# Macaron block on one core: query weights made in halves, the last batch's sums on two engines, fewer filler matmuls

## The chip, the cores and the metric

The kernel runs on one core of one Trainium2 chip. The metric is the device time of one execution in microseconds, lower is better; of a kernel the median of its runs is given. The names of the engines are those of the profile: PE is TensorE, DVE VectorE, ACT ScalarE, POOL GpSimd, SP the engine that only starts transfers. Each engine works through its own list of instructions in order and waits on semaphores for the others.

## What is computed

The input x is 16 batches of 512 rows of 128 numbers in float32. Three sublayers follow each other, each with a residual:

```
x = x + 0.5 * ffn(layernorm(x))      # one 128x128 weight, rounded to int4, plus a rank-16 term and a bias
x = x + attention(layernorm(x))
x = x + 0.5 * ffn(layernorm(x))      # the same weights again

attention: q = x Wq (16 heads of 64);  c = x Wkv_down (32 wide);  k = c Wk_up;  v = c Wv_up
           softmax(q k' / 8, causal) v, then Wout
```

Since k is c times a matrix of 64 columns per head, q k' is x (Wq Wk_up') c'. The kernel makes the product Wq Wk_up' once per head (128 x 32), the "query weights", and likewise Wv_up Wout. Scores are then products with only 32 contracted latents.

## The kernel before

**Rounds.** Every engine runs `one_round(t)` for t = -2 to 16. A round has up to four parts: `prep` makes the first sublayer, queries and keys of batch t+2; `top` finds row maxima of batch t+1; `attend` does scores and exponentials of batch t; `end` does the rest of batch t-1 (normalising, output projection, last sublayer, store). A round is cut into 44 slots u (`SCORES`), one score tile each. The order inside a round is written out by hand: the tables at the top of the file (`WEIGH_AT`, `ADD_AT`, `PROJECT_AT` and so on) give the slot at which an engine comes to each piece; a number over 43 lies in the next round. Rounds -2 and -1 have no scores, so only semaphores pace them; they use the `OPENING_` tables. In round 14 and later no new batch is prepared, round 15 attends the last batch, and round 16 only ends it.

**The opening.** PE rounds and centres the int4 weight (L780, then `w_ffn` by DVE, L1068). `front_unit(0)` transposes x of batch 0 (L929), ACT copies it (L718), `front_unit(1)` multiplies by `w_ffn` (L932), DVE adds the residual (L1202). Then `transpose_weights` transposes Wq and Wk_up in 8 pairs (L786, L787), ACT's `keep_transposed` copies them to SBUF (L663, L664), `query_products` multiplies (L796), and DVE's `keep_queries` scales them into `w_query` (L1074), makes a rounded copy `query_high` (L1078) and the remainder `query_low` (L1079). ACT fills rows of the query stack with the causal mask (`mask_queries`, L656): two groups at the start, one ahead of `keep_transposed`, one behind it; then it normalises x (`normalise`, L710). `front_unit(2)` transposes the normalised x (L929), ACT and DVE split it in `x_high` and `x_low` (L1221); `front_unit(3)` makes the keys and `front_unit(4)` to `(7)` the queries of the four groups of heads, three matmuls each (L941 to L943). POOL meanwhile fills `keys` with masks (L508, L522). In round -1 follow the next batch's first units, the value weights (L804, L812) and the first maxima (L903, with DVE's L1127).

**A batch's attention.** The 16 heads are four groups g of 4; a group has four key tiles j. PE makes scores (L839, L843), ACT takes exponentials (L697) into `first_probs` (j = 0) or `later_probs`. `weigh_latents(g, j)` multiplies them with the latents (L868); with j = 0 it first adds the row sums of the first 128 queries (L852). The other row sums come from `totals`, the sum of the probabilities over j: three adds per group, of 1536, 1024 and 512 columns, and `weigh_ones(g)` sums them over the partitions (L852). The adds of a batch run on POOL (`add_probs`, L593), those of the last batch all on DVE (`last_add`, L1144). An exponential that overwrites a buffer waits for the add that read it two groups before; `weigh_ones` waits for its group's three adds. ACT copies a group's result out of PSUM (`read_y`, L703).

**A batch's end.** When all four `weigh_ones` are done DVE inverts the sums (L1156), spreads them (L1163, in round 16 L1173) and POOL multiplies (`scale_y`, L600, four times; in round 16 `close_y`, L582, and DVE L1178). `project_out` (L985) waits for all of it, then come x2 (L1209, in round 16 L1183 and L1189), its transposes (`tail_unit(1)`, L998), the copy (L751), the last product (`tail_unit(2)`, L1001), POOL's bias and deviation (L637, L550, L552), and DVE's last sum (L1216) ahead of the store.

**Filler.** In round 16 PE also runs matmuls whose result nobody reads: `stay_busy_by_columns(BUSY[0])` ahead of each `weigh_ones` there (L969), `stay_busy(BUSY[1])` ahead of the first projection, `BUSY[2]` ahead of `tail_unit(1)`, `BUSY[3]` ahead of `tail_unit(2)` (L962); each of them is two matmul instructions of 256 columns.

Of the kernel before, what the change touches and what calls it, by code (L numbers as in the profile page):

```python
# [11 lines left out]
P = 128  # L12
# [123 lines left out]
LAST_WEIGH_AT = [[12, 17, 17, 17], [31, 31, 31, 31], [37, 37, 37, 37], [44, 49, 52, 65]]  # L136
LAST_ONES_AT = [31, 40, 44, 46]
# [56 lines left out]
def ones_at(b, g):  # L194

    return (LAST_ONES_AT if b == B - 1 else ONES_AT)[g]


def macaron_block(nc, x, wq, wkv_down, wk_up, wv_up, wout, ffn_w, ffn_bias, ffn_a, ffn_b, out):
    ctx = ExitStack()  # L200
    with ctx:
# [73 lines left out]
        w_query = early[:, 0:H * LD].rearrange("p (j o c) -> p j o c", o=2, c=LD)  # L275
# [6 lines left out]
        ring, (aux, score0, score1, y_bank, den_bank) = banks[:RING], banks[RING:]  # L282
        wide_scores = [*ring, score1, score0]
# [198 lines left out]
        def _(pool):  # L482
# [59 lines left out]
            def one_round(t, par):  # L542
# [59 lines left out]
                for u in range(SCORES):  # L602
# [10 lines left out]
                    for off, there in ((-1, end), (0, attend)):  # L613
                        for g in range(G):
                            for turn, at in enumerate(ADD_AT[g]):
                                if there and t + off < B - 1 and at == u - SCORES * off:
                                    add_probs(off, g, turn + 1)
# [25 lines left out]
        def _(act):  # L643
# [15 lines left out]
            def keep_transposed():  # L659

                act.wait_ge(w_pe, 4)
                for i in range(2):
                    nc.scalar.activation(wq_t[:, i * 4:(i + 1) * 4, :].rearrange("p j d -> p (j d)"), ring[i][:], ACT.Copy)  # L663
                nc.scalar.activation(wk_t[:].rearrange("p j c -> p (j c)"), ring[2][:, 0:H // 2 * LD],  # L664
                                     ACT.Copy).then_inc(w_act, 1)

            def keep_values():

                act.wait_ge(w_pe, 6)
                nc.scalar.activation(wv_t[:].rearrange("p j c -> p (j c)"), score1[:, 0:H // 2 * LD],  # L670
                                     ACT.Copy).then_inc(w_act, 1)
                act.wait_ge(w_pe, 7)
# [8 lines left out]
            def one_round(t, par):  # L681
# [62 lines left out]
                for u in range(SCORES):  # L744
# [23 lines left out]
        def _(pe):  # L768
# [9 lines left out]
            pe.wait_ge(w_dve, 3)  # L778
            pe.wait_ge(const_made, 6)
            nc.tensor.matmul(score1[:, 0:D], centering[:], quant[:, 1], start=True, stop=True).then_inc(w_pe, 1)  # L780

            def transpose_weights():
# [508 lines left out]
```

## Time and profile before

| | |
|---|---|
| median of 3 runs | 799.28 us (798.09 to 802.14) |
| profiled execution | 799.71 us |
| its span, first to last instruction | 797.5 us |
| PE busy | 764.4 us, 96% |
| DVE busy | 637.3 us, 80% |
| POOL busy | 628.1 us, 79% |
| ACT busy | 509.3 us, 64% |
| mean granted PE clock | 0.988 |

The engines' rows give the time in which each had an instruction running. Idle time of an engine costs only where the chain of waits that ends last goes through it. In the page's 40 slices of 20 us PE shows 9 in nearly all, and less in the first four and in the last two.

### The profile page before, as it was taken

The page shows a single profiled execution, that of the slowest core. Times are in us where ns is not written, and L with a number is a line of the kernel's source. Part 1 is how long each engine was busy: PE and PEld are TensorE (multiplying, and loading weights), DVE is VectorE, ACT ScalarE, POOL GpSimd, SP SyncE. Part 2 cuts the span into 40 slices and gives each one's busy share as a digit, 9 for nine tenths or more (in the row PEclk, how much of TensorE's full clock was granted, in tenths as well). Part 3 has the DMA queues.
Part 4 walks back from the last instruction along what each step waited for, and adds up shares of the span by engine and source line. Part 5 has one row for each costly group of instructions (what it writes and reads, how often), then busy time and mean ns, then how long its engine had stood idle before and what let it go on. Part 6 is the DMA issues. An engine that isn't in the chain of part 4 may idle for free.

```text
span 797.5 us, 20469 instructions
## 1 busy us (share of the span) xinstructions
PE 764.4 (96%) x7520; PEld 587.4 (74%) x7520; DVE 637.3 (80%) x1988; ACT 509.3 (64%) x993; POOL 628.1 (79%) x436
## 2 busy tenths in 40 slices
PE   5689999999999999999999999999999999999897
PEld 3556778778787777778787877878777877857576
DVE  3488878797878878897888879887888888876765
ACT  4365766667657666766757666776767666755660
POOL 4503879888998989888998989889898988878712
PEclk9988999999999999999999999999999999999999
DMA  4457272553627164453616264363626254360101
GB/s 115 95 124 174 53 158 72 120 128 81 162 49 161 46 147 101 107 143 81 154 41 157 65 140 108 89 160 74 148 50 154 72 125 112 81 141 2 29 2 41
DMA packets 81123, 80.97 MB, mean 102 GB/s; under 512 B 16048, under 2 KB 68544, under 8 KB 81024
## 3 DMA queue, kind: packets, MB, share of 16 engines
q1 hardware_dynamic: 80464, 78.47, 42.3%
q10 hardware_dynamic: 560, 1.20, 0.6%
q8 instruction: 60, 0.98, 0.5%
q14 instruction: 39, 0.32, 0.1%
HBM read 9.90 MB, written 8.39 MB: 23 GB/s over the span
## 4 chain that ended last, share of the span: by engine, by line
PE 85%; DVE 6%; SPq 2%; POOL 2%; ACT 2%; issue 2%; DMA 1%; ACTq 0%; DVEq 0%; POOLq 0%
PE bank L868 17%; PE bank L903 15%; PE bank L843 14%; PE bank L839 8%; PE bank L852 8%; PE bank L985 8%; PE bank L941 2%; PE bank L929 2%; SPq L398 2%; PE bank L943 2%; PE bank L942 2%; PE bank L932 2%; PE bank L1001 2%; DVE strip_max L1127 1%; PE bank L946 1%
## 5 line engine op out<-in xcount | busy, mean ns | idle before, releaser
L1127 DVE TENSOR_REDUCE strip_max<-bank 128x8 f32<-128x512 f32 (+1 forms) x384 | 254.2, 683 | 49.2 <-PE bank L903 48.5
L697 ACT ACTIVATE later_probs<-bank 128x512 f32<-128x512 f32 x384 | 216.3, 600 | 67.6 <-PE bank L843 41.9
L697 ACT ACTIVATE first_probs<-bank 128x384 f32<-128x384 f32 (+1 forms) x320 | 157.4, 512 | 139.7 <-PE bank L843 73.8
L593 POOL TENSOR_TENSOR totals<-totals,later_probs 128x1024 f32<-128x1024 f32 x120 | 220.2, 1835 | 11.5
L593 POOL TENSOR_TENSOR totals<-first_probs,later_probs 128x1536 f32<-128x1536 f32 x60 | 208.7, 3478 | 23.0 <-ACT later_probs L697 23.0
L903 PE MATMUL bank<-keys,q_stack 118*128 118x512 f32 (+7 forms) x1024 | 214.9, 304 | 3.0 <-DVE maxima L1127 1.2
L903 PEld LDWEIGHTS bank<-keys,q_stack 118*128 118x128 f32 x1024 | 177.7, 192 | 18.3 <-DVE strip_max L1127 3.7
L843 PE MATMUL bank<-q_stack,keys 119*128 119x384 f32 (+1 forms) x448 | 186.1, 424 | 2.8 <-ACT later_probs L697 1.7
L1127 DVE TENSOR_REDUCE maxima<-bank 128x1 f32<-128x512 f32 (+1 forms) x192 | 128.1, 681 | 3.9 <-PE bank L903 3.9
L843 PEld LDWEIGHTS bank<-q_stack,keys 119*128 119x128 f32 x448 | 83.6, 190 | 45.6 <-ACT first_probs L697 16.2
L839 PE MATMUL bank<-q_stack,keys 119*128 119x256 f32 x512 | 113.8, 304 | 0.9 <-DMA q_stack<-max_t 0.7
L839 PEld LDWEIGHTS bank<-q_stack,keys 119*128 119x128 f32 x512 | 82.7, 190 | 28.8 <-ACT later_probs L697 16.1
L868 PE MATMUL bank<-later_probs,lat 128*32 128x384 f32 (+2 forms) x1536 | 98.8, 383 | 0.0
L600 POOL TENSOR_TENSOR y_norm<-y_sb,y_norm 128x512 f32<-128x512 f32 x60 | 79.1, 1328 | 20.5 <-DVE y_norm L1163 20.5
L868 PEld LDWEIGHTS bank<-later_probs,lat 128*32 128x32 f32 x1536 | 43.6, 109 | 54.3 <-issue 35.5
L985 PE MATMUL bank<-w_out,y_norm 128*128 128x128 f32 x512 | 70.0, 281 | 2.9 <-POOL y_norm L600 2.4
L985 PEld LDWEIGHTS bank<-w_out,y_norm 128*128 128x128 f32 x512 | 64.5, 194 | 6.1 <-issue 5.3
L868 PE MATMUL bank<-first_probs,lat 128*32 128x512 f32 x512 | 66.7, 592 | 0.2 <-ACT y_sb L703 0.2
L1163 DVE STREAM_SHUFFLE y_norm<-den_inv 128x128 f32<-128x128 f32 x240 | 54.3, 308 | 0.5
L1231 DVE TENSOR_TENSOR q_low<-bank,q_high 128x512 fp32r<-128x512 f32 x64 | 43.8, 684 | 9.3 <-ACT q_high L729 9.2
L703 ACT ACTIVATE y_sb<-bank 128x512 f32<-128x512 f32 x64 | 38.4, 600 | 19.6 <-PE bank L868 19.6
L852 PE MATMUL bank<-totals,row_ones 128*32 128x128 f32 x1536 | 50.9, 273 | 0.0
(144 smaller groups left out, 889.9 us busy)
## 6 DMA issues: line engine op xcount, KB each, us to landing
q_stack<-q_high SPq DMA_DIRECT2D x252, 128.0 KB, 2.4
q_stack<-q_low SPq DMA_DIRECT2D x128, 128.0 KB, 2.4
x_in<-in_L_attn_x_bld_dram SPq DMA_DIRECT2D x16, 256.0 KB, 3.5
out_dram<-x SPq DMA_DIRECT2D x16, 256.0 KB, 3.5
x_back<-out_dram SPq DMA_DIRECT2D x16, 256.0 KB, 3.1
out_dram<-x2b SPq DMA_DIRECT2D x16, 256.0 KB, 2.3
keys<-keys_staged SPq DMA_DIRECT2D x16, 192.0 KB, 2.9
keys<-keys_staged SPq DMA_DIRECT2D x32, 96.0 KB, 2.8
```

The costliest lines, as they stand in the source:

```text
L593: nc.gpsimd.tensor_tensor(total, first_probs[g % 2][:, :, P:] if j == 1 else total, probs_of(g, j)[:], ALU.add).then_inc(added, 1)
L600: nc.gpsimd.tensor_tensor(y_norm[:, g, :], y_sb[:, g, :], y_norm[:, g, :], ALU.mult).then_inc(y_normed, 1)
L697: nc.scalar.activation(out, score_bank(t, u)[:, 0:heads * cols].rearrange("p (e q) -> p e q", e=heads), ACT.Exp).then_inc(exp_done, 1)
L839: last = nc.tensor.matmul(out, strips(par, KM, OWN[w]), q_stack[par][:, pair:pair + HG, w, of, :], start=True, stop=True)
L843: last = nc.tensor.matmul(bank[:, 0:heads * (n - P)], strips(par, KM, LATER[j]), q_stack[par][:, pair + e:pair + e + heads, 2 * (j + 1):SU ...
L852: last = nc.tensor.matmul(den_bank[e * LD:(e + 1) * LD, 0:P], row_ones[:, row:row + LD], of[:, e, :], start=start, stop=stop)
L868: last = nc.tensor.matmul(y_bank[e * LD:(e + 1) * LD, j * P:L], lat[(par + off) % 2][:, j, :], probs_of(g, j)[:, e, 0:L - P * j], start=(j ...
L903: last = nc.tensor.matmul(bank[:, col:col + n], queries, strips((par + off) % 2, KC, SEEN[w]), start=True, stop=True)
L985: last = nc.tensor.matmul(out_tile(t, i), y_norm[:, g, i * P:(i + 1) * P], w_out[:, g, :], start=(g == 0), stop=(g == G - 1))
L1127: nc.vector.tensor_reduce(out, bank[:].rearrange("q (b k) -> q b k", k=strip), AX.X, ALU.max).then_inc(a_free, 1)
L1163: last = nc.vector.stream_shuffle(y_norm[:, g, i * P:(i + 1) * P], den_inv[:], [g * TT + i] * LD)
L1231: nc.vector.tensor_tensor(q_low[:, g // 2, :, g % 2, :], front_bank(t, QUERY_UNIT + g)[:].rearrange("p (w q) -> p w q", q=HALF_TILE), q_hi ...
```

## The change

Three edits, none of which touches rounds 0 to 14.

In the opening the weights are transposed, copied, multiplied and kept in two halves of four pairs, the products in other banks; `w_query` is gone, `query_high` and `query_low` are both computed from PSUM; the centring matmul is issued behind `front_unit(0)`; and ACT fills both remaining mask groups ahead of the first copy. In the last batch the adds of groups 0 and 1 go to POOL, those of groups 2 and 3 stay on DVE, and the slots of adds, `weigh_latents` and `weigh_ones` are other ones. In round 16 `BUSY[2]` is 0 instead of 9.

```diff
-LAST_WEIGH_AT = [[12, 17, 17, 17], [31, 31, 31, 31], [37, 37, 37, 37], [44, 49, 52, 65]]
-LAST_ONES_AT = [31, 40, 44, 46]
+LAST_WEIGH_AT = [[10, 13, 13, 14], [21, 21, 25, 31], [33, 40, 40, 40], [42, 51, 52, 52]]
+LAST_ONES_AT = [33, 40, 52, 54]
...
-LAST_ADD_AT = [[19, 19, 22], [24, 24, 24], [30, 30, 32], [32, 41, 41]]
-BUSY = [1, 6, 9, 1]
+LAST_ADD_AT = [[10, 22, 22], [22, 24, 25], [28, 29, 34], [40, 40, 42]]
+BUSY = [1, 6, 0, 1]
+POOL_GROUPS = 2
...
+        product_banks = [(y_bank, den_bank), ring[0:2]]
...
-                                if there and t + off < B - 1 and at == u - SCORES * off:
-                                    add_probs(off, g, turn + 1)
+                                if there and (t + off < B - 1 or g < POOL_GROUPS) and u - SCORES * off == add_at(t + off, g, j):
+                                    add_probs(off, g, j)
...
-                            mask_queries(0, EARLY_MASKS)
-                            keep_transposed()
-                            mask_queries(0, EARLY_MASKS + 1)
+                            for g in range(EARLY_MASKS, G):
+                                mask_queries(0, g)
+                            keep_transposed(0)
...
+                    if is_first(t) and u == norm_at[TT - 1]:
+                        keep_transposed(1)
...
                     if is_first(t) and u == 1:
+                        centre_weights()
                         pe.wait_ge(w_dve, 4)
...
-                        pe.wait_ge(w_dve, 6)
+                        pe.wait_ge(w_dve, 6 + (u - QUERY_UNIT) // 2)
...
                     if is_first(t) and u == front_at[1]:
-                        transpose_weights()
-                        query_products()
+                        for half in range(2):
+                            transpose_weights(half)
+                        query_products(0)
+                    if is_first(t) and u == front_at[2]:
+                        query_products(1)
...
+            def keep_queries(half):
+
+                dve.wait_ge(w_pe, 6 + half)
+                js = slice(half * HG, (half + 1) * HG)
+                of = [bank[:, 0:HG * LD].rearrange("p (j c) -> p j c", c=LD) for bank in product_banks[half]]
                 for odd in range(2):
-                    ins = nc.vector.tensor_scalar(w_query[:, :, odd, :], ...
+                    last = nc.vector.tensor_scalar(query_high[:, js, odd, :], of[odd], HD ** -0.5, None, ALU.mult)
+                link(last)
+                for odd in range(2):
+                    last = nc.vector.scalar_tensor_tensor(query_low[:, js, odd, :], of[odd], HD ** -0.5,
+                                                          query_high[:, js, odd, :].bitcast(F32), ALU.mult, ALU.subtract)
...
                     if j == 1:
-                        wait_batch(dve, den_done, t, off, G, max(g - 1, 0))
-                    else:
-                        wait_batch(dve, added, t, off, G * GROUP_ADDS, g * GROUP_ADDS + j - 1)
+                        wait_batch(dve, den_done, t, off, G, g - 1)
+                    wait_batch(dve, added, t, off, G * GROUP_ADDS, g * GROUP_ADDS + j - 1)
```

On DVE `keep_queries(0)` stands where `keep_queries` stood, behind `split_keys`; `keep_queries(1)` stands behind the subtraction that finishes the keys (L1226) and ahead of the first `q_low`.

## Rows read from the trace of the kernel before

**Rows 1.** The page, busy time of each engine over the whole span.

```profile
PE 764.4 (96%) x7520; PEld 587.4 (74%) x7520; DVE 637.3 (80%) x1988; ACT 509.3 (64%) x993; POOL 628.1 (79%) x436
```

**Rows 2.** Timeline of the opening: start us, us, engine, line, operation; idle before in brackets.

```profile
8.92 0.29 DVE L1068 TENSOR_SCALAR w_ffn<-bank 128x128 f32<-128x128 f32 x1 [0.89 <-PE bank L780]
...
10.51 2.05 PE L932 MATMUL bank<-w_ffn,x_t 128*128 128x128 f32 x8 [0.78 <-ACT x_t L718]
...
12.60 1.13 DVE L1202 SCALAR_TENSOR_TENSOR x<-bank,f_rstd,x_in 128x128 f32<-128x128 f32 x4 [3.39 <-PE bank L932]
...
17.23 0.31 PE L787 MATMUL bank<-identity,y_sb 32*128 32x32 f32 x1
...
18.96 1.91 ACT L656 ACTIVATE q_stack<-first_probs 22x2048 fp32r<-22x2048 f32 x1
...
18.99 3.62 PE L796 MATMUL bank<-later_probs 64*128 64x32 f32 x32 [1.45 <-ACT later_probs L664]
20.89 1.65 ACT L710 ACTIVATE xn<-x,f_shift,f_rstd 128x128 f32<-128x128 f32 x4
...
21.78 3.75 POOL L522 MEMSET keys<- 22x2176 f32 x2
...
23.45 2.37 DVE L1078 CAST query_high<-later_probs 128x512 fp32r<-128x512 f32 x1
...
27.30 0.71 PE L941 MATMUL bank<-x_high,wkv_low 128*96 128x512 f32 x1 [3.63 <-DVE x_low L1221]
...
29.51 0.63 PE L943 MATMUL bank<-x_low,query_high 128*128 128x512 f32 x1
...
32.05 0.40 PE L943 MATMUL bank<-x_low,query_high 128*128 128x512 f32 x1
```

**Rows 3.** The same timeline further on, the first maxima on PE.

```profile
42.50 3.87 PE L903 MATMUL bank<-keys,q_stack 118*128 118x512 f32 x12
```

**Rows 4.** Timeline of the last batch, rounds 15 and 16.

```profile
746.84 2.28 ACT L697 ACTIVATE later_probs<-bank 128x512 f32<-128x512 f32 x4 [1.11 <-PE bank L843]
...
748.59 7.50 POOL L600 TENSOR_TENSOR y_norm<-y_sb,y_norm 128x512 f32<-128x512 f32 x4 [4.02 <-DVE y_norm L1163]
...
752.85 3.79 DVE L1144 TENSOR_TENSOR totals<-totals,later_probs 128x1024 f32<-128x1024 f32 x2
...
756.24 1.13 PE L985 MATMUL bank<-w_out,y_norm 128*128 128x128 f32 x8 [2.37 <-POOL y_norm L600]
...
758.41 2.02 DVE L1144 TENSOR_TENSOR totals<-totals,later_probs 128x1024 f32<-128x1024 f32 x2
...
763.95 1.04 PE L868 MATMUL bank<-first_probs,lat 128*32 128x512 f32 x8
...
778.79 1.48 PE L868 MATMUL bank<-later_probs,lat 128*32 128x384 f32 x24
779.04 0.96 DVE L1156 RECIPROCAL den_inv<-bank 128x128 f32<-128x128 f32 x1 [0.70 <-PE bank L852]
```

**Rows 5.** Windows: us, busy (instructions) PE, PEld, DVE, ACT, POOL, granted clock, DMA share, GB/s.

```profile
758.00:760.00 2.00, 2.00 (x10) 2.00 (x9) 1.79 (x3) 0.58 (x2) 0.00 (x0) 0.50 0.00 0
```

**Rows 6.** Groups of POOL by shape: busy us, mean ns, then idle before and its releaser.

```profile
L593 POOL TENSOR_TENSOR totals<-first_probs,later_probs 128x1536 f32<-128x1536 f32 x60 | 208.7, 3478 | 23.0 <-ACT later_probs L697 23.0
L593 POOL TENSOR_TENSOR totals<-totals,later_probs 128x1024 f32<-128x1024 f32 x60 | 143.0, 2383 | 4.9
L600 POOL TENSOR_TENSOR y_norm<-y_sb,y_norm 128x512 f32<-128x512 f32 x60 | 79.1, 1328 | 20.5 <-DVE y_norm L1163 20.5
L593 POOL TENSOR_TENSOR totals<-totals,later_probs 128x512 f32<-128x512 f32 x60 | 77.2, 1287 | 6.6
```

**Rows 7.** The chain of waits at the end: start us, us, what.

```profile
787.42 3.89 PE bank L962 x18
791.30 0.45 PE bank L998 x4
```

**Rows 8.** Timeline of the end, POOL and DVE.

```profile
789.37 1.04 POOL L552 TENSOR_TENSOR t_rstd<-t_var,neg_half 128x4 f32<-128x4 f32 x1
...
793.62 1.12 DVE L1216 SCALAR_TENSOR_TENSOR x2b<-bank,t_rstd,x2b 128x128 f32<-128x128 f32 x4 [5.03 <-PE bank L1001]
```

More of the change, by code:

```diff
@@ L614, in one_round @@
                         for g in range(G):
-                            for turn, at in enumerate(ADD_AT[g]):
-                                if there and t + off < B - 1 and at == u - SCORES * off:
-                                    add_probs(off, g, turn + 1)
+                            for j in range(1, TT):
+                                if there and (t + off < B - 1 or g < POOL_GROUPS) and u - SCORES * off == add_at(t + off, g, j):
+                                    add_probs(off, g, j)
                     if prep and u == rstd_at:
@@ L777, in _, with centre_weights, transpose_weights, query_products @@
             nc.tensor.matmul(score1[:, 0:1], ones[0:1, :], absmax[0:1, 2:3], start=True, stop=True).then_inc(w_pe, 1)
[L778 to L782, printed above, removed]
-                pe.wait_ge(w_loaded, 2 * DMA)
-                for j in range(H // 2):
-                    nc.tensor.transpose(ring[j // 4][:, (j % 4) * P:(j % 4 + 1) * P], wq_in[:, j * P:(j + 1) * P], identity[:])
-                    last = nc.tensor.transpose(ring[2][:, j * LD:(j + 1) * LD], wk_in[:, j * P:(j + 1) * P], identity[0:LD, 0:LD])
+            def centre_weights():
+                pe.wait_ge(w_dve, 3)
+                pe.wait_ge(const_made, 6)
+                nc.tensor.matmul(score1[:, 0:D], centering[:], quant[:, 1], start=True, stop=True).then_inc(w_pe, 1)
+            def transpose_weights(half):
+                pe.wait_ge(w_loaded, 2 * DMA)
+                q_bank, k_bank = (ring[0], ring[2]) if half == 0 else (ring[1], score0)
+                for n in range(HG):
+                    j = half * HG + n
+                    nc.tensor.transpose(q_bank[:, n * P:(n + 1) * P], wq_in[:, j * P:(j + 1) * P], identity[:])
+                    last = nc.tensor.transpose(k_bank[:, n * LD:(n + 1) * LD], wk_in[:, j * P:(j + 1) * P], identity[0:LD, 0:LD])
                 last.then_inc(w_pe, 1)
-            def query_products():
-                pe.wait_ge(w_act, 1)
-                for j in range(H // 2):
+            def query_products(half):
+                pe.wait_ge(w_act, half + 1)
+                for n in range(HG):
                     for odd in range(2):
                         rows = slice(odd * HD, (odd + 1) * HD)
-                        last = nc.tensor.matmul(ring[odd][:, j * LD:(j + 1) * LD], wq_t[rows, j, :], wk_t[rows, j, :],
-                                                start=True, stop=True)
+                        last = nc.tensor.matmul(product_banks[half][odd][:, n * LD:(n + 1) * LD], wq_t[rows, half * HG + n, :],
+                                                wk_t[rows, half * HG + n, :], start=True, stop=True)
                 last.then_inc(w_pe, 1)
@@ L1259, in one_round @@
                         for g in range(G):
-                            for turn, at in enumerate(LAST_ADD_AT[g]):
-                                if there and t + off == B - 1 and u - SCORES * off == at:
-                                    last_add(off, g, turn + 1)
+                            for j in range(1, TT):
+                                if there and t + off == B - 1 and g >= POOL_GROUPS and u - SCORES * off == add_at(t + off, g, j):
+                                    last_add(off, g, j)
             rounds(dve, one_round)
```

34 lines of the change are left out of this document (15 added, 19 removed).

## The prediction

> **What bounds the kernel now.** I read the page's busy shares first, then the chain of waits at both ends, then the timeline there with all engines side by side, and the windows for the clock. PE is busy 96% of the span [rows 1], and the middle, rounds 0 to 14, is left alone by the change. So the question is only the first 42 us, up to the first maxima [rows 3], and the last 50. In the opening the chain changes engines at each step, so a step saved there moves all that follows. The reader is to see in [rows 2] that PE waits 1.45 us for ACT's copies ahead of the products, that ACT then fills a mask (18.96 to 20.87) while the normalisation stands behind it, and that DVE has `query_high` in hand for 2.37 us beside POOL's memset; only then come x_low and, after 3.63 us of PE's waiting, the keys. In the last batch PE waits 2.37 us for POOL's scalings [rows 4] and then works at half clock, 0.50 (1.2 instead of 2.4 GHz) in the window of [rows 5]; behind that it has no gap until the inversion at 779.04. At the very end 18 filler matmuls stand on the chain for 3.89 us [rows 7].
>
> **Part 1, the opening.** I count from start to start.
> (a) Today x is transposed behind the centring matmul, and L932 starts at 10.51, released by the copy of x. In the new order the transposes stand in front of it, in a gap where PE waits for DVE; the copy is over by about 8.4, since ACT's first two masks end at 7.7. The next one late is `w_ffn`, ready at 9.21 [rows 2]. So L932 starts at 9.3: 1.2 us saved, and ends at 11.35.
> (b) The eight transposed pairs end at 17.54, which is 4.98 behind the end of L932 (12.56). They are not fewer: 11.35 + 5.0 = 16.35. ACT has done both masks by 8.4 + 2 x 1.91 = 12.2, ahead of the end of the first half at 13.6, so moving the second mask forward is free, and the first half's copies (about 0.9) lie beside PE's second half. PE goes straight on: first products 1.8 (half of 3.62), to 18.2; transposes of x about 1.0, to 19.2. The normalised x is there, because the mask no longer stands in front of it: its inputs come 1.2 earlier than today's 17.3, so 16.1 + 1.65 = 17.8. The second half's copies come behind it, 0.9, to 18.7; second products 1.8, to 21.0.
> (c) DVE keeps the first half at 18.2 with four instructions of 128 columns. The trace has no such instruction from PSUM into these buffers; L1202 has the same operation and width at 0.28 a step, L1068 is 0.29, the upper bound is the whole of today's 0.77 + 2.37 + 0.69 = 3.8 for both halves. I take 0.29 each, 1.2 with the link: done at 19.4, ahead of x_high (19.9). x_low ends at 20.6. So the keys start at 21.0 instead of 27.30: 6.3 us. With the upper bound (1.9 per half) x_low is over at 20.8, and nothing changes here.
> (d) The keys take 1.3 (PE) + 0.2 + 0.6 (ACT) + 0.7 (DVE), and only then DVE keeps the second half: 23.8 + 1.2 = 25.0. The third and fourth group's queries wait for it. Six matmuls of 512 columns follow at 0.43 to 0.24 each, depending on the clock: today they are 0.43 apart (0.63 long) until 30.4 and 0.24 apart (0.40 long) behind it [rows 2]. That is the end at 27.6 or at 26.5, against 32.45 today: 4.8 to 5.9 saved. I take 5.4. Bounds: 3.5, if the second half costs 1.9 and PE is still cold; 6.3, the gain at the keys.
> The Trainium skill says in "TensorE: Matmul & The Clock Gate", Part 1, that the slow clock is the default and steady activity releases it; by that rule the unbroken run of PE from 19.2 on would bring the fast clock by the queries (the 5.9 end), while from the rows alone I keep the middle.
> (e) Who is late next: from there ACT's last q_high, its four DMA issues, the latents' copy, the next batch's two units, the value weights and the first maxima [rows 3] follow each other as today. POOL's masks begin with the deviation, 1.2 earlier, and end at 27.7 instead of 28.9; they are needed ahead of the first maxima at 37. The loaded weights have landed (Wk_up, the later, near 9.7) ahead of the first transpose near 10.9. The transfers of queries and keys move with their sources. I let the 5.4 pass in full: rounds -1 and later have the same work in the same order.
>
> **Part 2, the last batch.** Before: DVE adds groups 0 and 1 beside POOL's scalings of batch 14. Four scalings take 7.50, 1.88 each against 1.33 on average [rows 4, 6], and DVE's adds of 1024 and 512 columns take 3.79 beside them, 2.02 without [rows 4]. So the two engines hold each other up.
> After, on POOL: the first add needs the exponential that ends at 747.45 (first of the four at 746.84 [rows 4]); 747.5 + 3.48, then four scalings of 1.28 to 1.33, is 756.1 to 756.3. That is where they end today (756.09): the add costs what the contention gives back. Then 2.38 + 1.29 for group 0 (760.0) and 3.48 + 2.38 + 1.29 for group 1 [rows 6]: 767.2. Behind the adds are queued the bias and the deviation of batch 14 (2.6, needed only at the round's last slots).
> On PE: `weigh_latents(1, 0)` and `(1, 1)` now stand in front of the projection. Their inputs come by 753.5 and 754.7 (ACT's order kept, 0.5 to 0.6 each), and they fill 0.35 + 0.86 + 0.64 = 1.85 of the wait. Against that `weigh_latents(3, 1..3)` now stand in front of the last sums instead of behind them (the 1.48 at 778.79 in [rows 4]): plus 1.43. The half clock: before, PE stood still 2.37 in one piece and was then at 0.50 for 3.41 us; half of this, 1.7, is lost time. After, what is left of the wait is about 1.3 in pieces. I take it that the clock stays up: minus 1.7. Sum: 779.04 - 1.85 + 1.43 - 1.7 + 0.1 (later projection) = 777.0, so 2.0 saved. Ends: 0.3 if the half clock stays, and 3.8 if the whole of the wait and of the clock were given back and the moved weighings cost nothing.
> Do the adds keep up? Group 1's sums are asked for on PE at about 769.2 and ready at 767.2: slack 2.0. Group 2's adds on DVE wait for POOL's last (767.2, since they now wait for the count) and run to 771.1; group 3's (1.76 + 2.02) wait for the exponentials of the round's end and run to 775.3, asked for at 776.3: slack 1.0. The end of batch 14 on DVE (L1216) comes behind them, off the chain.
> The Trainium skill has the rule for this in "SBUF — State Buffer", Who interferes with whom: a DVE instruction with two SBUF inputs and a GpSimd instruction that reads SBUF exclude each other for whole instructions. It agrees with the 3.79 against 2.02 above; it speaks against sharing one batch's sums between these two engines, and would matter here only for POOL's 1.29 bias add beside DVE's group 2, which has slack.
>
> **Part 3, the filler.** Behind x2 (DVE, 787.74) PE's transposes would start at 787.8 and not at 791.3 [rows 7]; copy, one filler, the last product: 787.8 + 0.6 + 0.7 + 1.2 = 790.3. Next late is POOL's deviation, which ends at 790.41 [rows 8]. DVE's last sum starts at 790.46 instead of 793.62: 3.15 saved. If the clock fell without the filler, the last product would take one more microsecond: 2.2. That is the lower end; there is no upper one beyond 3.15, as POOL sets it.
>
> **Sum.** 5.4 + 2.0 + 3.15 = 10.5 against the profiled execution, whose 799.71 is the span 797.5 and 2.2 around it: 789.2. That execution lies 0.43 over the median, so for a median 788.7. I say 789.0.
>
> **Rivals.**
> R1, the half clock stays in the last batch, or comes at another place of the rounds whose clock the shift disturbs: 1.7 less, 790.7. For it: PE still has gaps from 753 to 756; against it: they are shorter than the 2.37 today.
> R2, the opening's gain goes into a new wait, say the copies or the second half's chain (keys, ACT, DVE, then the kept half): only (a) and what the mask costs today, some 1.2 + 1.4, are left. 789.0 + 2.8 = 791.8. For it: the second half's queries hang on a chain of four engines; against it: PE's own work up to the keys, 21.0, is counted whole.
> R3, the last batch gives nothing, because its sums now end behind the weighings and their adds: 791.0.
> R4, the other side: POOL sets the pace of the last batch. Its adds of two groups are 14.3 us. If DVE's reads held POOL up as the scalings held up DVE (3.79 against 2.02, 1.88 times), they would take 26.9, 12.6 more; past the slack of 2.0 all of it is on the chain through the exponentials of group 3 and the sums: 10.6 more, and a PE that waits that long comes back at half clock, 1.7 more. 789.0 + 12.3 + the 2.0 not gained = 803.3; it begins to cost at 2.0 us of lateness and makes the kernel slower than before from about 12. Against it: between 756 and 767 DVE has little with two inputs in SBUF now.
> R5, both clocks fall out well and the queries take the 5.9: 786.5 to 788.
>
> **How the numbers follow.** Forecast 0.48, R1 0.16, R2 0.12, R3 0.08, R4 0.04, R5 0.08, and 0.04 for no gain that can be told. About 0.5%, 4 us, is what a measurement can tell from no change, so faster means below 795.3. The range takes in R1, R2, R3, R5 and combinations of two of the low ends (opening 3.5 and half clock: 792.7): 785.5 to 794.0. Faster 0.90, same 0.06, slower 0.04.
>
> **What would show it.** Keys' L941 near 21 and the last query matmul by 26.5 to 27.6; normalisation at about 16.2; no long CAST on DVE; the first L903 near 37. In the last batch: four L600 of about 1.3 each, L985 at the same distance from the round's start as now, no 0.50 in the windows behind it, L1156 about 2.0 nearer to it. At the end no L962 ahead of L998, and L1216 started by POOL's L552. The prediction is wrong if the first maxima come less than 3.5 us earlier, or if PE is seen waiting for adds (L593 or L1144) in round 15.

## The result and the profile after

The changed kernel took 789.95 us in the median of its runs (788.35 to 792.54) against 799.3 us, a ratio of 0.9881 with a 95% interval of 0.9843 to 0.9920. Run again later beside more runs of the kernel before, it gave 0.9910 (0.9888 to 0.9932). The forecast was 789.0 us in a range of 785.5 to 794.0. The profiled execution took 789.15 us, its span is 787.4 us; they are 10.6 and 10.1 below those of the kernel before. One of the ten runs of opening_only below took 4030.57 us and is left out of its ratio.

The line numbers moved: L932 is now L946, L796 is L809, L941 to L943 are L955 to L957, L903 is L916, L843 and L839 are L856 and L852, L868 is L881, L852 (sums) is L865, L593 is L599, L600 is L606, L1144 is L1161, L1156 is L1173, L985 is L999, L998 is L1012, L1216 is L1233.

The opening in the timeline of the changed kernel (start us, us, engine, line, operation; idle before in brackets), to be held against [rows 2]:

```profile
9.22 2.08 PE L946 MATMUL bank<-w_ffn,x_t 128*128 128x128 f32 x8 [0.38 <-DVE w_ffn L1085]
...
13.73 0.60 ACT L670 ACTIVATE later_probs<-bank 128x512 f32<-128x512 f32 x1 [1.64 <-PE bank L800]
...
16.06 1.65 ACT L717 ACTIVATE xn<-x,f_shift,f_rstd 128x128 f32<-128x128 f32 x4 [1.56 <-POOL f_shift L575]
...
16.21 1.92 PE L809 MATMUL bank<-later_probs 64*128 64x32 f32 x16
...
18.17 0.49 DVE L1093 TENSOR_SCALAR query_high<-bank 128x128 fp32r<-128x128 f32 x2 [3.49 <-PE bank L809]
18.70 0.49 DVE L1096 SCALAR_TENSOR_TENSOR query_low<-bank,query_high 128x128 fp32r<-128x128 f32 x2
19.11 1.92 PE L809 MATMUL bank<-later_probs 64*128 64x32 f32 x16
...
20.96 0.74 PE L955 MATMUL bank<-x_high,wkv_low 128*96 128x512 f32 x1
...
26.26 0.40 PE L957 MATMUL bank<-x_low,query_high 128*128 128x512 f32 x1
```

L946 now waits for `w_ffn` and no longer for the copy of x. The first half's copy (13.73) lies beside the second half's transposes, PE goes from them to the first products without waiting, and neither the second products nor the keys (20.96) have a wait in brackets: from 16.2 to the keys PE is its own limit. DVE has kept the second half at 24.94, and the third group's queries start behind it at 24.99, after a wait of 0.22. The last query matmul ends at 26.66 instead of 32.45. Further on, the first maxima, to be held against [rows 3]:

```profile
36.64 4.17 PE L916 MATMUL bank<-keys,q_stack 118*128 118x512 f32 x12
```

The last batch, to be held against [rows 4]:

```profile
740.97 2.28 ACT L704 ACTIVATE later_probs<-bank 128x512 f32<-128x512 f32 x4 [1.11 <-PE bank L856]
...
741.65 3.50 POOL L599 TENSOR_TENSOR totals<-first_probs,later_probs 128x1536 f32<-128x1536 f32 x1 [2.94 <-ACT later_probs L704]
...
745.11 5.00 POOL L606 TENSOR_TENSOR y_norm<-y_sb,y_norm 128x512 f32<-128x512 f32 x4
...
748.67 1.04 PE L881 MATMUL bank<-first_probs,lat 128*32 128x512 f32 x8
749.53 0.83 PE L881 MATMUL bank<-later_probs,lat 128*32 128x384 f32 x8
...
750.29 1.16 PE L999 MATMUL bank<-w_out,y_norm 128*128 128x128 f32 x8
...
761.38 2.73 DVE L1161 TENSOR_TENSOR totals<-first_probs,later_probs 128x1536 f32<-128x1536 f32 x1 [3.15 <-POOL totals L599]
...
768.23 2.02 DVE L1161 TENSOR_TENSOR totals<-totals,later_probs 128x1024 f32<-128x1024 f32 x2
...
772.03 0.96 DVE L1173 RECIPROCAL den_inv<-bank 128x128 f32<-128x128 f32 x1 [0.74 <-PE bank L865]
```

The four scalings take 5.00, not 7.50, and end at 750.1 with the first add of 3.50 in front of them. Counted from batch 14's inversion (746.45 before, 740.58 after) the projection starts at +9.79 before and at +9.71 after: the same place. The last inversion is at +32.59 before and +31.45 after. The windows after the projection (us, then busy us of PE, PEld, DVE, ACT, POOL, granted clock, DMA share, GB/s), against [rows 5]:

```profile
752.00:754.00 2.00, 2.00 (x20) 1.34 (x19) 0.00 (x0) 1.53 (x4) 1.86 (x3) 1.00 0.00 0
754.00:756.00 2.00, 2.00 (x19) 2.00 (x19) 0.00 (x0) 1.02 (x3) 2.00 (x1) 1.00 0.00 0
```

And the end, against [rows 8]:

```profile
782.34 1.04 POOL L558 TENSOR_TENSOR t_rstd<-t_var,neg_half 128x4 f32<-128x4 f32 x1
783.51 1.12 DVE L1233 SCALAR_TENSOR_TENSOR x2b<-bank,t_rstd,x2b 128x128 f32<-128x128 f32 x4 [1.94 <-POOL t_rstd L558]
```

PE is no longer the one that DVE's last sum waits for; POOL's deviation is. From inversion to that sum it is 11.48 now, 14.58 before.

By milestones of the two profiles the 10.1 us of span are: 5.9 up to the first maxima (5.5 at the first score of batch 0, 65.20 against 59.66, and 5.9 at batch 14's inversion), 1.1 in the last batch, 3.1 at the filler.

### The profile page after: what moved, and what is told of

Its sections match the earlier page's. It is cut to its first block, busy times and chain, and to the rows that moved or that the text cites. A ratio compares the mean times of both kernels' runs of the same rounds, so it can differ in the third digit from the quotient of the medians.

```text
span 787.4 us, 20439 instructions
## 1 busy us (share of the span) xinstructions
PE 762.5 (97%) x7502; PEld 583.2 (74%) x7502; DVE 626.7 (80%) x1986; ACT 509.3 (65%) x994; POOL 642.0 (82%) x442
## 4 chain that ended last, share of the span: by engine, by line
PE 88%; DVE 5%; ACT 2%; POOL 1%; issue 1%; SPq 1%; DMA 1%; ACTq 0%; POOLq 0%; DVEq 0%
PE bank L881 18%; PE bank L916 16%; PE bank L856 14%; PE bank L852 8%; PE bank L865 8%; PE bank L999 7%; PE bank L955 2%; PE bank L943 2%; PE bank L956 2%; PE bank L957 2%; PE bank L946 2%; PE bank L1015 2%; DVE strip_max L1145 1%; SPq L404 1%; PE bank L960 1%
## 5 line engine op out<-in xcount | busy, mean ns | idle before, releaser
L599 POOL TENSOR_TENSOR totals<-totals,later_probs 128x1024 f32<-128x1024 f32 x124 | 227.3, 1833 | 11.9
L599 POOL TENSOR_TENSOR totals<-first_probs,later_probs 128x1536 f32<-128x1536 f32 x62 | 215.7, 3479 | 25.9 <-ACT later_probs L704 25.9
L916 PE MATMUL bank<-keys,q_stack 118*128 118x512 f32 (+7 forms) x1024 | 215.2, 305 | 2.5 <-DVE maxima L1145 1.2
L916 PEld LDWEIGHTS bank<-keys,q_stack 118*128 118x128 f32 x1024 | 178.5, 193 | 17.4 <-DVE strip_max L1145 2.8
L856 PE MATMUL bank<-q_stack,keys 119*128 119x384 f32 (+1 forms) x448 | 185.8, 423 | 2.7 <-ACT later_probs L704 1.7
L856 PEld LDWEIGHTS bank<-q_stack,keys 119*128 119x128 f32 x448 | 83.0, 189 | 45.7 <-ACT first_probs L704 16.0
L852 PE MATMUL bank<-q_stack,keys 119*128 119x256 f32 x512 | 114.1, 305 | 0.3 <-ACT later_probs L704 0.2
L852 PEld LDWEIGHTS bank<-q_stack,keys 119*128 119x128 f32 x512 | 82.6, 190 | 29.9 <-ACT later_probs L704 17.2
L881 PE MATMUL bank<-later_probs,lat 128*32 128x384 f32 (+2 forms) x1536 | 99.5, 383 | 0.0
L606 POOL TENSOR_TENSOR y_norm<-y_sb,y_norm 128x512 f32<-128x512 f32 x60 | 76.5, 1287 | 16.6 <-DVE y_norm L1180 16.6
L881 PEld LDWEIGHTS bank<-later_probs,lat 128*32 128x32 f32 x1536 | 43.1, 109 | 54.2 <-issue 35.3
L999 PE MATMUL bank<-w_out,y_norm 128*128 128x128 f32 x512 | 69.1, 278 | 1.5 <-POOL y_norm L588 1.5
L999 PEld LDWEIGHTS bank<-w_out,y_norm 128*128 128x128 f32 x512 | 63.1, 191 | 5.9 <-issue 3.8
L881 PE MATMUL bank<-first_probs,lat 128*32 128x512 f32 x512 | 66.7, 592 | 0.3 <-ACT y_sb L710 0.2
L865 PE MATMUL bank<-totals,row_ones 128*32 128x128 f32 x1536 | 50.9, 273 | 0.0
L736 ACT ACTIVATE q_high<-bank 128x512 fp32r<-128x512 f32 x64 | 38.4, 599 | 16.5 <-PE bank L957 16.2
```

Of the source, the lines that this page charges most:

```text
L599: nc.gpsimd.tensor_tensor(total, first_probs[g % 2][:, :, P:] if j == 1 else total, probs_of(g, j)[:], ALU.add).then_inc(added, 1)
L606: nc.gpsimd.tensor_tensor(y_norm[:, g, :], y_sb[:, g, :], y_norm[:, g, :], ALU.mult).then_inc(y_normed, 1)
L852: last = nc.tensor.matmul(out, strips(par, KM, OWN[w]), q_stack[par][:, pair:pair + HG, w, of, :], start=True, stop=True)
L856: last = nc.tensor.matmul(bank[:, 0:heads * (n - P)], strips(par, KM, LATER[j]), q_stack[par][:, pair + e:pair + e + heads, 2 * (j + 1):SU ...
L865: last = nc.tensor.matmul(den_bank[e * LD:(e + 1) * LD, 0:P], row_ones[:, row:row + LD], of[:, e, :], start=start, stop=stop)
L881: last = nc.tensor.matmul(y_bank[e * LD:(e + 1) * LD, j * P:L], lat[(par + off) % 2][:, j, :], probs_of(g, j)[:, e, 0:L - P * j], start=(j ...
```

## The experiments

Each edit is against the kernel before or the changed one, as it says. A ratio is that of its runs to runs of the kernel before on the same chip.

**opening_only**: the changed kernel with the last batch's tables, its adds' engine and the fillers put back.

```diff
-BUSY = [1, 6, 0, 1]
+BUSY = [1, 6, 9, 1]
-POOL_GROUPS = 2
+POOL_GROUPS = 0
...                # and LAST_WEIGH_AT, LAST_ONES_AT, LAST_ADD_AT as before
```

> The kernel with the opening's edits alone; last batch and filler as before. Theory (each engine step moved what follows): the first maxima start at 36.6, 5.9 earlier than 42.5, the first score of batch 0 5.5 earlier, and the span is 797.5 - 5.5 = 792.0. Rival (the rounds behind give part of it back, through transfers or another clock pattern in rounds -1 and 0): first maxima as above, but a span above 794.5. Third possibility, that part of the gain seen at the end of the changed kernel is not the opening's: span under 791.

Measured: 795.02 us, ratio 0.9943 (0.9919 to 0.9967), which is 4.5 us (2.6 to 6.5). In its profile the first maxima start at 38.01 and the first score at 62.76, the span is 794.4: 1.4, 3.1 and 2.4 us later than expected. Up to the keys it was all as in the changed kernel (below). What differs is the clock: the table further down shows 22.4 us at half clock up to that score in this profile against 11.5 in the changed kernel's. So I had taken the accident of one pair of profiles for the size of the term. The profiled run is also the longest of the nine that count, and the record, which has a mean granted clock for every run, shows the same link in all of them: they go from 796.65 us at 0.981 to 791.80 us at 0.991.

**last_batch_only**: the kernel before with the last batch's three tables, POOL's adds of groups 0 and 1, and DVE's additional wait.

> The kernel with the last batch's edits alone (adds of groups 0 and 1 on POOL, the new slots of weighings and sums), opening and 9 fillers as before. Theory: POOL's scalings take 5.0 instead of 7.5 and end where they ended; the half clock behind the projection is gone; the inversion starts 1.1 to 1.4 earlier (between batch 14's and the last inversion 31.2 to 31.5 instead of 32.6). Rival, that the gain of 1.1 in the changed kernel is the shifted clock windows and not the new order: then here the half clock stays, and the distance is over 32.3.

Measured: 798.04 us, ratio 0.9977 (0.9957 to 0.9996), 1.8 us (0.3 to 3.4). The inversions are 31.47 apart (744.65, 776.12), no half clock behind the projection, scalings 5.00. As the theory had it.

**filler_only**: the kernel before with `BUSY = [1, 6, 0, 1]`.

> The kernel with BUSY[2] = 0 alone: 9 filler matmuls less ahead of the last transposes. Theory: DVE's last sum is released by POOL's deviation and starts 3.1 earlier (from inversion to last sum 11.5 instead of 14.6), PE's clock stays at 1.00 to the last product; span 794.4. Rival, that PE drops to half clock without the fillers and the last product ends behind POOL: 12.4, span 795.3.

Measured: 796.26 us, ratio 0.9949 (0.9929 to 0.9969), 4.1 us (2.5 to 5.7). From inversion to last sum 11.50, the clock at 1.00 from round 1 until 792.7. The chain of waits of this run (start us, us, what) shows who took over; in [rows 7] it was 3.89 of PE's fillers:

```profile
786.78 0.83 POOL x2b L637
787.61 0.41 issue
788.02 0.23 POOL t_var L550
788.25 0.04 issue
788.29 1.09 POOLq L201
```

This run held a surprise elsewhere. Its last batch is that of the kernel before, to the instruction, with the same wait of 2.37 ahead of the projection, and yet the clock did not fall behind it:

```profile
756.81 1.13 PE L985 MATMUL bank<-w_out,y_norm 128*128 128x128 f32 x8 [2.37 <-POOL y_norm L600]
757.70 0.48 PE L839 MATMUL bank<-q_stack,keys 119*128 119x256 f32 x2
758.01 1.05 PE L985 MATMUL bank<-w_out,y_norm 128*128 128x128 f32 x8
```

The second projection takes 1.05 here and 1.85 in the profile of before:

```profile
757.45 1.85 PE L985 MATMUL bank<-w_out,y_norm 128*128 128x128 f32 x8
```

Here the clock stays at 1.00, and the inversions are 30.98 apart (747.02, 778.00) instead of 32.59. So the half clock costs 1.6 us there, and it is not in every run.

**slots_only**: the kernel before with the new slots of weighings and sums, all adds left on DVE.

```diff
-LAST_WEIGH_AT = [[12, 17, 17, 17], [31, 31, 31, 31], [37, 37, 37, 37], [44, 49, 52, 65]]
-LAST_ONES_AT = [31, 40, 44, 46]
+LAST_WEIGH_AT = [[10, 13, 13, 14], [21, 21, 25, 31], [33, 40, 40, 40], [42, 51, 52, 52]]
+LAST_ONES_AT = [33, 40, 52, 54]
```

> The kernel with the new slots of weighings and sums in the last batch, but all adds on DVE at their old slots. It tells the two edits of the last batch apart. Theory (contention): POOL's scalings still take about 7.5 beside DVE's adds, the projection starts at the same place, and since the wait is filled with the two weighings here too, the half clock goes and the inversion comes 1 to 1.4 earlier: the adds' new engine is worth nothing by itself. Rival, that moving the adds to POOL is what counts: the distance between the two last inversions stays at 32.3 to 32.6 here.

Measured: the scalings take 7.53, the projection is 9.81 behind the inversion, the next inversion 31.52 (749.26, 780.78), against 31.45 and 31.47 with the adds on POOL. Between the inversions the engine of the adds is worth nothing by itself. The whole took 800.1 us, ratio 0.9999 (0.9978 to 1.0019), so in the median the slots alone show no gain. That is 2.1 us more than last_batch_only, more than the last batch of the two profiles can explain. A part is the clock: seven of these ten runs have a mean of 0.981 to 0.985, only three of the ten of last_batch_only 0.982 to 0.984, and in both kernels the runs with the lower clock are mostly the longer ones. Whether the rest is chance or the adds' engine, no run here shows.

**psum_read_only**: the kernel before, `query_high` and `query_low` made from PSUM in one piece.

```diff
-                    ins = nc.vector.tensor_scalar(w_query[:, :, odd, :],
...
-                link(nc.vector.tensor_copy(query_high[:], w_query[:]))
-                nc.vector.tensor_tensor(query_low[:], w_query[:], query_high[:].bitcast(F32),
...
+                    last = nc.vector.tensor_scalar(query_high[:, :, odd, :], of[odd], HD ** -0.5, None, ALU.mult)
...
+                    last = nc.vector.scalar_tensor_tensor(query_low[:, :, odd, :], of[odd], HD ** -0.5,
+                                                          query_high[:, :, odd, :].bitcast(F32), ALU.mult, ALU.subtract)
```

> Of the opening only this: DVE makes query_high and query_low from PSUM, in one piece, so no copy or cast between SBUF buffers is left. In the profile of before the cast took 2.37 us beside POOL's memset, in three later profiles of the same code 0.51. Theory (the cast and the memset exclude each other, and who comes first at the memset's end decides): the four instructions take 1.5 to 1.7 in all, the keys' first matmul starts 2.9 to 3.1 behind the end of the products, as in the runs in which the cast won (3.0) and not as before (4.7); in the median a gain of 0 to 1 us, within the noise. Rival, that reading from PSUM is itself slow or also held: the four instructions take over 2.5, keys start over 4 behind the products.

The long cast of [rows 2] had turned out to be an accident too. In last_batch_only, slots_only and filler_only, whose opening is that of the kernel before, it is short. The last of them, in its timeline:

```profile
21.98 4.04 POOL L522 MEMSET keys<- 22x2176 f32 x2
22.88 0.75 DVE L1074 TENSOR_SCALAR later_probs<-bank 128x256 f32<-128x256 f32 x2 [6.72 <-PE bank L796]
23.66 0.51 DVE L1078 CAST query_high<-later_probs 128x512 fp32r<-128x512 f32 x1
24.21 0.69 DVE L1079 TENSOR_TENSOR query_low<-later_probs,query_high 128x512 fp32r<-128x512 f32 x1
```

POOL's two memsets start at 21.98 and about 23.85. The cast starts at 23.66, inside the first. Here it gets its turn between the two: it takes 0.51, and POOL's pair takes 4.04. In the kernel before the second memset came first: cast 2.37, pair 3.75. In both the cast starts 0.23 to 0.24 before the end of the first memset (1.91 each), so the times do not show what decides. Measured with psum_read_only: 0.76 + 0.76 for the four instructions, the keys 2.55 behind the end of the products (23.39 to 25.94; I had expected 2.9), ratio 0.9986 (0.9964 to 1.0008), not to be told from no change.

**order_only**: the kernel before, with the centring behind the transposes of x and both mask groups ahead of the copies.

> Of the opening only the orders: centring matmul behind the transposes of x, both mask groups ahead of the copies; weights in one piece, kept through w_query as before. Theory: L932 starts at 9.3 (1.2 earlier) and the normalisation about 16.1 to 16.5 or right behind the copies at 18.5, but the products still end at 21.4 and the keys start 24.2 to 24.5 (against 25.65 in runs without the long cast): 1.2 to 1.4 us. Rival, that the mask's place was the chief cost: 2 us or more.

Measured: the start of the whole moves by up to 1.2 us between runs (the first data land differently), so the opening is read from DVE's first instruction, which waits for them (3.82 to 4.99 in the runs here). From it to the keys it is 20.29, against 21.50 with the cast short: 1.21, that is the centring's place. The mask's place adds nothing here, where the products of the weights in one piece end at 22.26 and the keys wait for what DVE does behind them; whether the mask behind the copies would hold up the halves was not tried. Ratio 0.9978 (0.9954 to 1.0001).

**fill_the_wait**: the kernel before, with unread matmuls in round 15's wait.

```diff
+                        if t == B - 1:
+                            for _ in range(5):
+                                nc.tensor.matmul(aux[:, 0:L // 2], identity[:], w_out[:, 0:2, :], start=True, stop=True)
```

> The kernel before plus ten filler matmul instructions of 256 columns (unread, into the output's bank) on PE in round 15 while it waits for the first projection. Theory (the 1.6 us between the last two inversions, 32.6 with and 31.0 without a half clock, are the clock alone): no 0.50 behind the projection, distance 31.0, end 1.6 earlier than in a run that has the half clock; the projection itself starts where it did. Rival, that fillers delay the projection or the clock falls all the same: 32.6 or more.

Measured: 2.32 of fillers, the projection at +9.72, no half clock, the inversions 30.93 apart (747.37, 778.30). Ratio 0.9981 (0.9962 to 1.0000), 1.5 us (0 to 3.0). With filler_only, which has neither the fillers nor the half clock and 30.98, it shows that the clock alone makes the 1.6, and that without it the old order is 0.5 us faster than the new one.

**all_on_pool**: the changed kernel with `POOL_GROUPS = 4`.

> The changed kernel with all twelve adds of the last batch on POOL. It prices the slack. Theory: POOL has group 1's adds by 761.2 and needs 7.15 per group more instead of 3.8: group 2's and the bias work end about 771, group 3's about 778.5 instead of 770.3, so the last sums wait and the inversion comes at about 779, 7 later than in the changed kernel: span 794 to 795. Rival, that the adds have more slack than I think: under 3 us later.

Measured: 799.11 us, ratio 0.9999 (0.9980 to 1.0018), span 796.3; the inversions are 39.33 apart, 7.9 more than in the changed kernel (7 expected). PE waits for the adds (who waited for whom, us in total, times, longest), and its clock falls behind it, from 776.1 for 6.8 us:

```profile
PE bank L865 <- POOL totals L599: 6.9, 1, 6.9
```

Two groups fit on POOL, four use up the whole gain of the change.

**after_again**: the changed kernel.

> The changed kernel once more, with more runs beside those of before. Theory (opening 4.5 in the median, since the long cast and the clock windows fall differently from run to run, last batch 1 to 2, filler 3.1): median 8.5 to 10 below before. The halves' milestones as in its first profile: keys at most 12.0 behind the start of L946, last two inversions 31.4 to 31.5 apart, inversion to last sum 11.5.

Measured: 792.12 us against 798.46, ratio 0.9910 (0.9888 to 0.9932), 7.2 us (5.4 to 8.9): below the 8.5 to 10 that I had expected, though the interval reaches into it. The three parts, each measured alone, add up to 10.4 (4.5, 1.8 and 4.1), and the first measurement of the whole gave 9.4; the intervals are too wide to say that the parts get in each other's way. Keys 11.73 behind L946, inversions 31.44 apart, 11.51 to the last sum. First score at 62.66, 3.0 later than in the first profile of the same program.

**no_sum_filler**: the changed kernel with `BUSY = [0, 6, 0, 1]`.

> The changed kernel with BUSY[0] = 0: the 16 filler matmul instructions of 0.86 us per group ahead of the last two weigh_ones are gone. Theory (the adds of group 3 on DVE have about 1.0 of slack to the last sums): of 1.7 only 1.0 comes back, then PE waits for L1161; inversions 30.4 to 30.5 apart, and 0.8 to 1.0 in the median. Rival, that without them the clock falls: 32 or more.

(A unit of `BUSY[0]` is eight matmul instructions of 512 columns, L983, once for each of the two groups; only the units of the other three are two of 256 columns.) Measured: 790.86 us, ratio 0.9891 (0.9869 to 0.9913), which can't be told from after_again by its interval; inversions 30.72 apart, 0.7 less, and PE waits 0.8 for L1161. The adds do limit, a little earlier than I had said.

**warm_opening**: the changed kernel, with unread matmuls in PE's waits of the opening.

```diff
+                    fill = {(-2, front_at[LATENT_UNIT]): 6, (-1, front_at[0]): 5, (-1, front_at[1]): 2}.get((t, u), 0)
+                    for _ in range(fill):
+                        nc.tensor.matmul(ring[2][:, 0:P], identity[:], identity[:], start=True, stop=True)
```

> The changed kernel with 13 unread matmuls of 128 columns on PE, into a free bank, in the three waits between the last query and the second unit of batch 1 (1.4, 1.2 and 0.7 us). Theory (the half clock of 31 to 41 us comes from PE standing still there, and costs what PE then does on the chain, some 2 us up to the first maxima): no 0.50 from 31 on, L946 of round -1 1.1 instead of 2.1, first maxima 1.5 to 2.5 nearer to the end of the queries (8.0 to 8.9 instead of 10.4), 1 to 2.5 in the median. Rival, that the clock falls all the same, or that DVE (which sets the pace of round -1) eats the gain: under 0.5 in the first score of batch 0.

Measured: 789.00 us, ratio 0.9884 (0.9862 to 0.9906). The median is 3.1 below after_again; the two intervals overlap, so the gain rests on the milestones. Windows of after_again (columns as above):

```profile
24.00:31.00 7.00, 4.16 (x14) 2.64 (x12) 5.05 (x17) 2.55 (x5) 4.13 (x13) 0.93 0.68 150
31.00:41.00 10.00, 8.67 (x60) 6.71 (x60) 4.18 (x16) 3.55 (x8) 3.72 (x6) 0.54 0.95 216
```

and of warm_opening:

```profile
24.00:31.00 7.00, 6.92 (x44) 5.72 (x42) 5.00 (x17) 2.85 (x6) 4.68 (x13) 1.00 0.68 150
31.00:41.00 10.00, 8.67 (x72) 5.99 (x70) 7.36 (x21) 6.11 (x12) 3.11 (x6) 0.89 0.95 213
```

The clock of the second is 1.00 in the first of the two windows and 0.89 in the other, where it was 0.54. (Its first entry is at 25.1, in after_again at 26.5. Ahead of that the views print 1.00 too, though PE's matmuls of 512 columns are 0.43 apart there, as at half clock, and 0.24 behind it.) In its timeline (PE) what follows the queries is short:

```profile
31.47 1.16 PE L946 MATMUL bank<-w_ffn,x_t 128*128 128x128 f32 x8 [0.24 <-ACT x_t L725]
33.71 1.08 PE L825 MATMUL bank<-y_norm,later_probs 64*32 64x128 f32 x32 [0.47 <-ACT later_probs L677]
34.72 1.05 PE L916 MATMUL bank<-keys,q_stack 118*128 118x512 f32 x5
```

The first maxima are 7.8 behind the last query matmul's end (26.96 to 34.72), in after_again 10.8 (27.55 to 38.37), where L946 of this round took 2.07 and L825 1.93. In all five profiles of this opening without the fillers it is 9.2 to 10.8, in the two with them 7.8 and 7.9. The fillers also bring the half clock to another place (from 38.7), so the first score comes only 2.5 earlier.

**both_more**: the two together.

> Both of these on the changed kernel: the sum of the two, 2 to 3.5 below after_again in the median, and the fastest of all kernels here.

Measured: 787.74 us (787.20 to 788.89), ratio 0.9864 (0.9842 to 0.9887): 4.4 below after_again, 2.2 below the changed kernel's first median, and the fastest kernel here. Its interval overlaps those of the two alone.

Milestones of the profiles, worked out from their timelines and windows ("keys": from DVE's first instruction to the first keys matmul; "clock": time at half clock between the first full clock and the first score of batch 0; "score": from the keys to that score; all in us):

```
kernel             cast   keys    clock   score
before             2.37   23.36    7.4    37.90
fill_the_wait      2.37   23.36   15.6    39.37
last_batch_only    0.51   21.50   10.2    37.66
filler_only        0.51   21.50   10.2    39.64
slots_only         0.52   21.50   22.3    42.03
psum_read_only     -      21.23   18.8    39.49
order_only         0.52   20.29   18.9    40.35
the change         -      17.06   11.5    38.70
opening_only       -      17.06   22.4    41.58
after_again        -      17.06   19.1    41.36
no_sum_filler      -      17.06   18.4    39.68
all_on_pool        -      17.06   15.6    40.37
warm_opening       -      17.06   11.1    38.82
both_more          -      17.05    5.0    37.32
```

Up to the keys a program repeats itself to 0.01 us, but for the cast; behind them nearly the same work takes 37.3 to 42.0, and mostly the longer the more of it lies at half clock.

## Why the prediction was right, and where it was lucky

**The opening up to the keys** was right step by step: L946 forecast 9.3, found 9.22; normalisation 16.1, found 16.06; first products over at 18.2, found 18.13; keys 21.0, found 20.96; the end of the queries between 26.5 and 27.6, found 26.66, with the clock rising among the queries, at 24.2. The third group's queries started at 24.99 (25.0 in step (d)). The unknown instructions, taken at 0.29, took 0.28 to 0.29 each, two of them 0.49 since they overlap. Step (b), that the mask's move is free, holds; that the mask was in the way of anything is not borne out, since order_only shows 1.21 for step (a) and nothing for the mask. Neither of the two signs of being wrong came: the first maxima are 5.9 earlier, and PE waits for no adds in round 15.

**What was wrong in it is the size.** Step (c) gave 6.3 at the keys by reading 27.30 in one profile. Six of the openings profiled had the old cast in them: in two it was long (keys at 23.36 from DVE's first instruction), in four short (21.50 with the old order). The change brings 17.06 always: 6.3 or 4.44, of which 1.21 is the order, 0.27 the reading from PSUM where the cast would have been short, and the remaining 2.96, by difference, the halves (no run has them alone). Step (e), that the gain passes on in full, holds for the work but not for the clock: in rounds -1 and 0 the stretches at half clock move by several microseconds from run to run. opening_only gives 4.5 (2.6 to 6.5) in the median; 5.4 was high but inside.

**The last batch.** That POOL's added work and the end of the contention cancel was right to 0.1 us, and slots_only shows it from the other side: with 7.53 of scalings the projection comes at the same place. That the filled wait keeps the clock up was right in all eight profiles with the new slots; with the old ones and no fillers it fell in four of five. And fill_the_wait shows that the clock is the cause of the 1.6 (1.7 forecast). The mis-sized term is the rest: -1.85 + 1.43 + 0.1 = -0.3 was forecast for the order itself; with the clock taken out it is +0.5 (31.45 against 30.93 and 30.98). So 2.0 was forecast for the last batch, and 1.1 came. (The upper end that the forecast gives it, 3.8, is not the sum of its own terms either: the wait of 2.37 and the clock's 1.7 are 4.1.) The chain of waits of the changed kernel shows where, among the last scores of group 2:

```profile
756.34 0.28 ACT later_probs L704
756.62 0.19 issue
756.81 0.02 ACTq L110
756.82 0.01 issue
756.83 0.64 ACT later_probs L704 x2
757.47 0.32 issue
757.78 0.63 ACT y_sb L710
```

Here the exponentials and the copy of y set the pace, not PE, and the 1.85 filled into the earlier wait do not come back. PE has some work beside these 2.1 us (L881, L852 and L865, 20 instructions); by their pieces elsewhere in the same chain it is 1.2, so about 0.9 is lost, an estimate, against the 0.8 by which the forecast is off. In the old order the weighings that now fill the wait stand at this place, and the chain of filler_only is PE's alone from the projection (756.81) to the inversion (778.00):

```profile
762.74 0.36 PE bank L852 x8
763.09 2.15 PE bank L868 x32
765.25 0.65 PE bank L852 x24
```

The forecast had added up PE's list without ACT's. So the change gains in the last batch only in runs in which the old kernel would have lost its clock. The slack of the adds (2.0 and 1.0) was about right: 763.45 for the sums of group 1 against their adds' end at 761.24, and 0.7 in no_sum_filler for the second.

**The filler.** 3.15 forecast, 3.10 in the changed kernel and 3.08 in filler_only; the next late engine was POOL, as named.

**Luck in the total.** 10.5 was forecast for the profiled execution and 10.6 found, 789.0 for the median and 789.95 found. By milestones that is 5.9 where 5.4 stood and 1.1 where 2.0 stood: two misses that cancel. The 5.9 holds 1.86 us of a cast that is long in two of six profiles, and the 1.1 is there only because the kernel before had a half clock that another run of the old order did not have. Beside more runs the gain is 7.2 us (5.4 to 8.9), well below the 10.3 between 799.3 and 789.0.

**The rivals.** R1 and R3 did not come whole, but each has a part: the clock did fall at other places of the opening, and the last batch's order gave nothing by itself. Of R2 there is only the 0.22 that PE waits for the kept second half. R5 came for the queries (5.8), not for the total. R4's mechanism exists: all_on_pool has it, without any contention, for adds that are too many. Its milder form is seen at 761.38, where DVE's add takes 2.73 beside POOL's bias and 1.76 alone:

```profile
761.20 1.29 POOL L643 TENSOR_TENSOR x2b<-x,half_bias 128x512 f32<-128x512 f32 x1
762.46 1.74 POOL L556 TENSOR_SCALAR t_var<-t_mv 128x4 f32<-128x4 f32 x1
766.37 1.76 DVE L1161 TENSOR_TENSOR totals<-first_probs,later_probs 128x1536 f32<-128x1536 f32 x1
```

The Trainium skill, "SBUF — State Buffer", Who interferes with whom, says that a DVE instruction with two SBUF inputs contends with a GpSimd instruction that reads SBUF, and the trace agrees: the add ends 1.62 behind the bias, and POOL's L556, 0.23 elsewhere, ends with the add.

## What to carry to other kernels

Read a milestone in several profiles before pricing a step from it: here a cast of 0.5 or 2.4 us and stretches of half clock moved single profiles by up to 4 us, nearly as much as the step itself was worth. When a wait is filled with work of its own engine, follow the other engines behind it; the work may only have changed places with a wait, and then unread matmuls in the gap do as well. Filler is paid for where it stands on the chain (3.1 us here), and can earn where PE stands still anyway.

## What the runs showed of the hardware

- A DVE cast between SBUF buffers that came up 0.23 us before the end of a POOL memset, with another memset behind it, took 0.51 or 0.52 us in four profiles and 2.37 in two. In five of the six the opening is the same code, with both outcomes. From PSUM the same values took 0.49 per pair of instructions in halves, and 0.76 in one piece, beside such memsets.
- Small POOL instructions beside DVE adds stretch too: in the changed kernel's round 15 L556 (4 columns) took 1.74 instead of 0.23, L558 2.05 instead of 1.04.
- The same wait of PE of 2.37 us was followed by 3.4 us at half clock in some runs (before, opening_only, psum_read_only, order_only) and by none in another (filler_only). The price was 1.6 us between the last two inversions.
- In the opening, from its first entry on, the granted clock lay at half (1.2 instead of 2.4 GHz) for 5 to 22 us up to the first score of batch 0; 13 unread matmuls in PE's waits took it away where they stood and moved it to a later place.
